# A decoder on one core: projection of the first attention in quarters and three units ahead, and another order of splits and additions in the last stage

## The reference

```
q, k = rope(x @ wq), rope(x @ wk)      # 16 and 4 heads of 128
v = x @ wv                             # 4 heads of 32
attn = softmax(q @ k.T / sqrt(128) + mask)
out = (attn @ v) @ wo
```

```
output = silu(x @ Ws1) * (x @ Wsg) @ Ws2
p = softmax(x @ gate_w + gate_b); top3 = top_k(p + biases, 3)
for e in range(7):
    output += (silu(x @ W1[e]) * (x @ Wg[e]) @ W2[e]) * w_e   # w_e: share of e in top3, or 0
```

## Time and profile before

| | us |
|---|---|
| median of 3 runs | 2308.58 (2304.91 to 2310.09) |
| profiled execution | 2314.31 |
| its span | 2312.2 |
| PE busy in the span | 1995.7 (86%) |
| DVE busy | 1452.0 (63%) |
| ACT busy | 1076.5 (47%) |
| POOL busy | 605.4 (26%) |
| mean granted TensorE clock | 0.939 |

### The profile page before, as it was taken

The page is one execution under the profiler, slowest core; times in us unless marked ns, Lnnn a source line. Parts: engine busy times, 40 slices in busy tenths (PEclk is TensorE's granted clock), DMA queues, the critical chain, the costliest instruction groups (busy, mean ns, idle before and its releaser), DMA issues. The chain is left out here.

```text
span 2312.2 us, 32930 instructions
## 1 busy us (share of the span) xinstructions
PE 1995.7 (86%) x11168; PEld 1201.7 (52%) x11168; DVE 1452.0 (63%) x2728; ACT 1076.5 (47%) x2150; POOL 605.4 (26%) x510
## 2 busy tenths in 40 slices
PE   6777776978999889996999999996698886699998
PEld 4454553446777567773545445453255543355553
DVE  5565565456775667766856667587699966445434
ACT  3555543222333323331635446371798893244332
POOL 3555520013332223320100101011644550132320
PEclk8999987988999889998999999997699998799999
DMA  4000003111110111104011010003700003467533
GB/s 134 24 24 1 1 1 114 37 48 46 46 45 0 58 36 46 45 0 133 21 30 43 19 36 18 0 1 65 175 1 2 1 1 109 136 184 179 145 72 88
DMA packets 95792, 125.26 MB, mean 54 GB/s; under 512 B 8926, under 2 KB 52254, under 8 KB 95662
## 3 DMA queue, kind: packets, MB, share of 16 engines
q1 hardware_dynamic: 88942, 107.79, 15.8%
q0 software_dynamic: 6720, 15.73, 3.6%
HBM read 101.68 MB, written 18.61 MB: 52 GB/s over the span
## 5 line engine op out<-in xcount | busy, mean ns | idle before, releaser
L1164 POOL TENSOR_TENSOR wl<-stage,wh 128x512 fp32r<-128x512 f32 x80 | 117.2, 1496 | 399.4 <-DVE wh L1155 399.4
L1423 POOL TENSOR_TENSOR Zl<-z,Zh 128x512 f16<-128x512 f32 x32 | 51.1, 1597 | 494.3 <-ACT Zh L1584 494.3
L1264 ACT ACTIVATE h<-PS,bup 128x512 f32<-128x512 f32 x64 | 44.2, 690 | 279.2 <-PE PS L79 279.2
L77 PE MATMUL PS<-XTh,wh 128*128 128x512 f16 x416 | 157.9, 380 | 0.5 <-DVE wl L1662 0.5
L78 PE MATMUL PS<-XTl,wh 128*128 128x512 f16 x416 | 157.9, 379 | 0.0
L79 PE MATMUL PS<-XTh,wl 128*128 128x512 f16 x416 | 157.7, 379 | 0.0
L2461 POOL TENSOR_TENSOR PTl<-P,PTh 128x512 f16<-128x512 f32 (+2 forms) x128 | 116.2, 918 | 124.6 <-ACT PTh L2633 124.5
L2632 ACT ACTIVATE P<-PS 128x512 f32<-128x512 f32 (+3 forms) x256 | 135.1, 528 | 21.7 <-PE PS L2558 19.8
L2633 ACT ACTIVATE PTh<-PS 128x512 f16<-128x512 f32 (+3 forms) x256 | 136.2, 532 | 0.0
L2648 DVE TENSOR_REDUCE M<-PS 128x1 f32<-128x640 f32 (+3 forms) x128 | 127.1, 1013 | 4.5 <-PE PS L2534 4.4
L2461 DVE TENSOR_TENSOR PTl<-P,PTh 128x512 f16<-128x512 f32 (+1 forms) x128 | 96.1, 756 | 50.0 <-ACT PTh L2633 48.7
(11 more groups left out here) (378 smaller groups left out, 5831.4 us busy)
## 6 DMA issues: line engine op xcount, KB each, us to landing
stage<-in_ffn_W SPq DMA_DIRECT2D x18, 1024.0 KB, 5.4
stage<-in_ffn_Wg SPq DMA_DIRECT2D x9, 1024.0 KB, 5.5
stage<-in_ffn_Wup SPq DMA_DIRECT2D x16, 512.0 KB, 3.9
stage<-in_ffn_Wdn SPq DMA_DIRECT2D x16, 512.0 KB, 3.6
wq<-in_attn_wq SPq DMA_DIRECT2D x4, 1024.0 KB, 5.5
C<-in_ctx SPq DMA_DIRECT2D x8, 512.0 KB, 8.8
stage<-in_ffn_Wsw SPq DMA_DIRECT2D x16, 256.0 KB, 3.6
stage<-in_attn_WV SPq DMA_DIRECT2D x16, 256.0 KB, 4.1
```

The costliest lines, as they stand in the source:

```text
L77: pe.matmul(out, a[0], b[0], start=start, stop=False, skip_group_check=True)
L1164: nc.gpsimd.tensor_tensor(piece(wl[q], ch), piece(st, ch), plain(piece(wh[q], ch)), ALU.subtract).then_inc(w_lo, 1)
```

## The change

In the first attention, `project(n)` becomes `project(n, k)`, a quarter of a tile. Each quarter (two, where a unit has two tiles to project) follows a score tile and its transpositions, for the tiles that unit u + 3 needs; before, whole tiles for unit u + 2 followed the fourth score tile. The first three units' tiles are projected ahead of the loop. ACT makes the high copies for unit u + 1 and the `halves` for unit u + 2 after exp 0 of unit u, the copies ahead of PTh and the halves behind it. DVE's `cosines` move behind the first maximum, with `outputs` for unit u - 2. POOL makes the low half of unit u + 1's tiles and then turns unit u + 2's. In the last stage the store of `rows` moves behind load 2; split 2 moves ahead of the router's exp on ACT and of `place` on DVE; splits 3 and 4 move between the shared expert's blocks; `name` and its matmuls move one block forward; two additions move ahead of split 5.

```diff
--- before.py
+++ after.py
@@ -766,7 +766,7 @@
         @block.sync
         def _(sp):
             for n in range(LOADS):
-                if n == 2:
+                if n == 3:
                     sp.dma_start(c.rows.rearrange("(t p) d -> p t d", p=P), c.X[:]).then_inc(rows_stored, 16)
                 e, i = divmod(n, 3)
                 need(sp, w_ready, n - 1)
@@ -888,8 +888,8 @@
             route.counts(pe)
             shared_up(0, 1, 0)
             shared_up(0, 2, 0)
+            route.name_tokens(pe)
             shared_up(0, 3, 0)
-            route.name_tokens(pe)
             pe.wait_ge(w_ready, 3)
             for q in range(QT):
                 shared_down(0, q, 0)
@@ -962,13 +962,14 @@
             split_hi(0)
             route.copy(act, 1)
             split_hi(1)
+            split_hi(2)
             route.exp(act)
-            split_hi(2)
             for m in range(KD):
                 silu(m, 2 * (m % 2))
                 shared_g(0, m)
-            for n in range(3, 6):
-                split_hi(n)
+                if m in (1, 2):
+                    split_hi(m + 2)
+            split_hi(5)
             x_high(0)
             for j in range(TILES):
                 silu(KD + j, 0)
@@ -1035,16 +1036,21 @@
             split_lo(0)
             split_lo(1)
             route.select(dve)
+            split_lo(2)
             route.place(dve, lambda: (g(0, 1), shared_low(0, 0)))
-            split_lo(2)
             for m in range(1, KD):
                 g(m, 2 * (m % 2) + 1)
                 shared_low(0, m)
-            route.name(dve)
+                if m == 1:
+                    split_lo(3)
+                if m == 2:
+                    route.name(dve)
+            split_lo(4)
             route.weigh(dve)
-            for n in range(3, 6):
-                split_lo(n)
-            for q in range(QT):
+            for q in range(2):
+                add_shared(0, q)
+            split_lo(5)
+            for q in range(2, QT):
                 add_shared(0, q)
             route.slot_weights(dve)
             x_low(0)
@@ -1792,7 +1798,7 @@
 
     def tiles(u):
 
-        if u >= N:
+        if not 0 <= u < N:
             return []
         first = u + u // REP + (1 if u % REP else 0)
         return [first, first + 1] if u % REP == 0 else [first]
@@ -1867,37 +1873,43 @@
         @block.gpsimd
         def _(pool):
             def rotate(n):
-                g, b, hh = tile(n)
-                q, u = n % 2, KVH * B * g + REP * b + hh - 1
-                hi, lo = (Kh[:, b, :], Kl[:, b, :]) if hh == 0 else (Qh[:, u % 2, :], Ql[:, u % 2, :])
+                q = n % 2
                 pool.wait_ge(a_half, 2 * n + 2)
                 nc.gpsimd.tensor_tensor(t2[:, q, :], t2[:, q, :], sin[:], ALU.mult).then_inc(r_sin, 1)
                 pool.wait_ge(r_sin, n + 1)
                 pool.wait_ge(a_cos, n + 1)
                 need(pool, r_lo, n - 1)
                 nc.gpsimd.tensor_tensor(r32[:, q, :], t1[:, q, :], t2[:, q, :], ALU.add).then_inc(r_sum, 1)
+
+            def low(n):
+                g, b, hh = tile(n)
+                u = KVH * B * g + REP * b + hh - 1
+                hi, lo = (Kh[:, b, :], Kl[:, b, :]) if hh == 0 else (Qh[:, u % 2, :], Ql[:, u % 2, :])
                 pool.wait_ge(r_hi, n + 1)
-                nc.gpsimd.tensor_tensor(lo, r32[:, q, :], hi, ALU.subtract).then_inc(r_lo, 1)
+                nc.gpsimd.tensor_tensor(lo, r32[:, n % 2, :], hi, ALU.subtract).then_inc(r_lo, 1)
 
             nc.gpsimd.memset(zero[:], 0.0).then_inc(zeroed, 1)
             nc.gpsimd.memset(Vh[:, :, :, DV:VW], XS).then_inc(ones_done, 1)
             nc.gpsimd.memset(Vl[:, :, :, DV:VW], 0.0).then_inc(ones_done, 1)
             pool.wait_ge(const_in, 48)
-            for u in range(N):
-                for n in tiles(u):
+            for u in range(-2, N):
+                for n in tiles(u + 1):
+                    low(n)
+                for n in tiles(u + 2):
                     rotate(n)
 
         @block.tensor
         def _(pe):
-            def project(n):
+            def project(n, k):
                 g, b, hh = tile(n)
-                pe.wait_ge(w_lo, (REP + 1) * g + hh + 1)
-                need(pe, a_half, 2 * (n - 1))
-                for k in range(KD):
-                    last = products(pe, c.PS[:, n % 2, :], (wh[:, g, hh, k, :], wl[:, g, hh, k, :]),
-                                    (c.XTh[:, k, b * S:(b + 1) * S], c.XTl[:, k, b * S:(b + 1) * S]),
-                                    start=(k == 0), stop=(k == KD - 1))
-                last.then_inc(a_done, 1)
+                if k == 0:
+                    pe.wait_ge(w_lo, (REP + 1) * g + hh + 1)
+                    need(pe, a_half, 2 * (n - 1))
+                last = products(pe, c.PS[:, n % 2, :], (wh[:, g, hh, k, :], wl[:, g, hh, k, :]),
+                                (c.XTh[:, k, b * S:(b + 1) * S], c.XTl[:, k, b * S:(b + 1) * S]),
+                                start=(k == 0), stop=(k == KD - 1))
+                if k == KD - 1:
+                    last.then_inc(a_done, 1)
 
             def scores(u, qt):
                 b = u // REP % B
@@ -1963,17 +1975,20 @@
                     last = products(pe, c.PS[:, 4 + t % 4, 0:KVH * DV], (c.XTh[:, k, tok], c.XTl[:, k, tok]),
                                     (wvh[:, k, :], wvl[:, k, :]), start=(k == 0), stop=(k == KD - 1))
                 last.then_inc(v_done, 1)
-            for n in tiles(0) + tiles(1):
-                project(n)
+            for n in tiles(0) + tiles(1) + tiles(2):
+                for k in range(KD):
+                    project(n, k)
             pe.wait_ge(v_lo, NT)
             pe.wait_ge(ones_done, 2)
             for u in range(N):
+                chunks = [(n, k) for n in tiles(u + 3) for k in range(KD)]
+                each = len(chunks) // QT
                 for qt in range(QT):
                     scores(u, qt)
                     if u > 0 and qt < NTU:
                         turn(u - 1, qt)
-                for n in tiles(u + 2):
-                    project(n)
+                    for n, k in chunks[each * qt:each * (qt + 1)]:
+                        project(n, k)
                 if u > 0:
                     values(u - 1)
             for j in range(NTU):
@@ -2024,21 +2039,20 @@
                 act.wait_ge(v_done, t + 1)
                 nc.scalar.activation(Vh[:, t, :, 0:DV], c.PS[:, 4 + t % 4, 0:KVH * DV].rearrange("p (g e) -> p g e", g=KVH),
                                      ACT.Copy, scale=1.0 / WS).then_inc(v_hi, 1)
-            halves(0)
-            halves(1)
-            rotated(0)
-            rotated(1)
-            halves(2)
+            for u in range(2):
+                for n in tiles(u):
+                    halves(n)
+                for n in tiles(u) if u == 0 else ():
+                    rotated(n)
             for u in range(N):
                 for qt in range(QT):
                     exp(u, qt)
-                    if qt == 2 and u + 1 < N:
-                        for n in tiles(u + 1):
-                            rotated(n)
+                    for n in tiles(u + 1) if qt == 0 else ():
+                        rotated(n)
                     if u > 0 and qt < NTU:
                         turned(u - 1, qt)
-                for n in tiles(u + 2):
-                    halves(n)
+                    for n in tiles(u + 2) if qt == 0 else ():
+                        halves(n)
             for j in range(NTU):
                 turned(N - 1, j)
             for t in range(NT):
@@ -2132,16 +2146,17 @@
                     maximum(u, qt)
                     if u > 0 and qt > 0:
                         turned(u - 1, qt - 1)
-                for n in tiles(u + 2):
-                    cosines(n)
-                if u > 0:
-                    outputs(u - 1)
-                for hh in {0: (0,), 1: (1,), 3: (2,), 4: (3,), 5: (4,)}.get(u % U, ()) if u < N - U else ():
+                    for n in tiles(u + 2) if qt == 0 else ():
+                        cosines(n)
+                    if u > 1 and qt == 0:
+                        outputs(u - 2)
+                for hh in {1: (0,), 2: (1,), 3: (2,), 4: (3,), 5: (4,)}.get(u % U, ()) if u < N - U else ():
                     weights(u // U + 1, hh)
                 if u == N - 3:
                     output_weights()
             for j in range(NTU):
                 turned(N - 1, j)
+            outputs(N - 2)
             z_part(0)
             z_part(1)
             outputs(N - 1)
```

## The result

The changed kernel takes 2270.44 us (median of four runs, 2268.35 to 2273.47), the kernel before on the same chip 2306.74 (2304.03 to 2310.09). The ratio is 0.9843 [0.9823, 0.9862]: 36.3 us faster. The forecast was 2262.5 in a range of 2244 to 2285, so the direction held and the gain of 46 was 10 too large.

A forecast was written before the change was run, and what follows sets the result against it. TensorE was taken to bound the attention loop, idle a quarter of the time behind DVE's PTl. Attention 34 + 7 - 4 = 37 us plus last stage 9 gave 46 off 2308.58: 2262.5 us, range 2244 to 2285.

The forecast's parts named there:

- The length of the units: First attention's loop: units of 6.4, 8.4, 9.3 and 6.8 us, 31.0 in four against 35.9; 34 us gained.
- the bank wait: First attention, units with u % 4 = 2: projection waits 2.7 us for ACT's halves to read its PSUM bank.
- The clock: First attention's loop: 4 us (0 to 10) charged against a sum made at full clock.
- rival 3: Attention: TensorE standing briefly in each unit could stay at 1.2 GHz, making the kernel slower, 2349 us; chance 4%.
- The ends of the loop: First attention: unit 1 starts about 3 us earlier, the end gives 4; 7 taken, between 0 and 8.
- Shared work of DVE and POOL: Attention loop: fifteen weight splits on DVE while POOL works could cost 0 to 13 us; 0 taken.
- The wait before products with V: One-tile units of the attention: about 0.6 us stays, derived from the last score tile's maximum and PTl.
- rival 1: Attention: halves before exp 1 in ACT's queue slow all one-tile units, bank wait 4.5; 2280 to 2285 us; chance 18%.
- The last stage: Up to the first routed tile: exp 5.0 us late, first addition 7.0 earlier; gain 9, bounds 2 and 12.
- the change of nothing (4): Whole kernel: no change within 0.2%; some 15 us won in the loop, 13 lost to DVE and POOL blocking; chance 3%.
- rival 5: Only the last stage fails, exp's 5 us not absorbed: 46 less 9, 2270 to 2274 us; chance 7%.
- Rival 2: Attention: waits all but go, four units approach 25.8 us; kernel at 2230 to 2245; chance 10%.

The follow-up runs named there:

- the mended projection: Changed kernel, but where u % 4 = 2 two quarters stand behind score tile 2 and two behind tile 3, none earlier; alone 2251.1 us, ratio 0.9744.
- the mended kernels: Changed kernel with late projection where u % 4 = 2 and exp ahead of split 2: 2245.42 us; also without a quarter behind tile 2 in other units: 2247.8.
- the mended version: Changed kernel with two quarters each behind score tiles 2 and 3 where u % 4 = 2, and exp ahead of split 2; 2245.42 us, ratio 0.9723.

## Why the prediction was right, and where it was wrong

*The length of the units* was right. Forecast 6.4, 8.4, 9.3 and 6.8 us; measured, where the clock stays up, 6.42, 8.33, 9.27 and 6.94. The wait before transpositions went, the bank wait came with 2.71 us (forecast 2.7), seven times, released by ACT's halves, in the unit named.

*The 10 us too many* (46 forecast, 36 measured) split up by the traces: 4.8 in the loop, 1.3 at its ends and 0.7 in the last stage, 6.8 in all. The other 3 lie within what the measurement can tell.

*The clock* is the mis-sized term. I charged 4 us for the loop. Four units last 10.94, 10.95, 12.20 and 10.64 in place of 9.27: 7.7 in the first profile, and with seven of seven about 4.5 more. The 28 units took 224.9 us in the first profile where the sum had 250.1 - 34 + 4 = 220, and 229.4 in the second. The reason for 4, that waits of 3 us remain only in every fourth unit, was true, but no row of mine priced a drawn-out unit. The price is 1.3 to 2.9 us for each, about half of the wait's own 2.71 or more. The trace of the kernel before has a lower one: six of its seven waits of 3.38 us have the low clock behind them, and in units with the same weight splits the four units from the wait at 182.66, with it, last 36.6 us, those from 111.19, without it, 35.3. There a part of the loss fell into time in which TensorE would have waited anyway: the next wait before transpositions, 0.83 us at 114.51, is gone at 186.60. The new order has little such time left. A summary of the clock, 0.95 before and 0.96 after, hid it: the share of slow time hardly fell, where the forecast had nearly full clock. The Trainium skill, "TensorE: Matmul & The Clock Gate", "A second HAM failure mode: psum-queue depth-cycling", stood behind rival 3, the kernel slower by its clock. The runs don't show a fall from cycling through banks alone: with the same banks in turn and waits of at most 1.43 us the granted clock is 1.00.

*The ends of the loop* were forecast at 7 and gave 5.7: unit 1 starts 2.9 us earlier (48.82 to 45.91, about 3 forecast), the tail is 2.8 shorter (4 forecast). One pair of traces doesn't fix this to better than 2 us: in the others with the new attention unit 1 starts at 44.1 to 46.3. A smaller slip is in the sum itself: 7 x 4.9 = 34, where the loop before was 250.1 and the four units gave 217, 33.

*Shared work of DVE and POOL*, costed at nothing, was nothing that shows: 28 units at the forecast lengths and the four drawn-out ones account for the loop within 0.3 us. DVE's split itself shows once the bank wait is mended: a unit with it is then 8.67 us instead of 7.65. How much of that comes from the two engines' sharing no run tells.

*The wait before products with V* had the right size by the wrong chain. I forecast 0.6 and derived it from the last maximum, which would begin 0.3 us behind its matmuls. It measured 0.48 to 0.69. But the maximum is ready and not waited for. DVE's timeline of the kernel after, unit 4:

```profile
76.10 0.56 DVE L2096 SCALAR_TENSOR_TENSOR PTl<-PS,PTh 128x384 f16<-128x384 f32 x1 [0.64 <-ACT PTh L2034]
76.58 0.55 DVE L2089 CUSTOM_DVE_ANT_0 Pr<-PS,mask 128x384 f32<-128x384 f32 x1
...
77.05 0.55 DVE L2096 SCALAR_TENSOR_TENSOR PTl<-PS,PTh 128x384 f16<-128x384 f32 x1
```

PTl 1 waits 0.64 for ACT, and maximum and PTl 2 follow without a gap; TensorE goes on at 77.66. The chain is rival 1's (halves ahead of exp 1), at the forecast's price, so that this figure came out right by luck. The kernel with no quarter behind tile 2 was made on the wrong chain and gained nothing. That a shorter stay of the halves in ACT's queue would shorten the wait wasn't tried.

*The last stage* was forecast at 9 and gave 8.3 in the profile, 5.3 to 12.2 alone. exp's delay was 5.9 instead of 5.0, the first addition 6.4 earlier instead of 7.0. From DVE's going on after exp to the first addition it is 38.6 us, where the sum had 39.3 + 5.7 - 6 = 39.0. The sum carried exp's delay in full, and rightly: with exp first again the stage is 5.5 to 7.0 us shorter. What the forecast didn't say is that the move could be left out: without it the first routed tile comes 13.6 to 15.3 us earlier than before, not 8.3. And the wait for the addition did not shrink to 2; it went, and 5.24 us came at the head of the same product. By the Trainium skill, "ScalarE: Activation LUTs", "What ACT_TABLE_LOAD costs", a drain of about 1.4 us would be added to each switch; the trace has 1.28 for the load at 1909.94 and exp right behind it at 1911.23, so no drain shows here. The load cost time for another reason: it stands behind a copy that waits 6.08 us for its transfer.

*Rivals.* The bank wait of 4.5 (rival 1) and the change of nothing (4) are excluded by the profile. Of rival 5 the condition came, exp's delay was not absorbed, but not its price: the other moves gave more than 9, and the stage still won 8.3. Rival 3's lasting fall didn't come, but part of its mechanism is what the forecast lacked. Rival 2, most waits gone, asked for a loop near four units in 26 us; the mended kernels, with 29.8, go less than a quarter of the way there from the 31.0 forecast, though their 2245 to 2248 lie near the upper end of its range, for they also have exp first.

Left open: why the same 2.71 us wait has the low clock behind it in four units of one execution, in five of others and in seven of yet others.

## What to carry to other kernels

Where in-order queues hand work round a loop, take the lead (how many units ahead, with the orders that belong to it) and the interleaving apart and price each. Here quarters alone moved the wait from one line to the next (0.9984), the lead with the new orders gave all that the whole change gave, and the mended version 64 us. Price a wait of TensorE with the clock it may cost behind it, the more so where little other waiting is left to take it up, and look for the bank that is taken too early. Put nothing that waits for a transfer ahead of a short instruction that another engine stands for.

## What the runs showed of the hardware

A TensorE wait of 2.71 us, once in about 31 us, was followed by matmuls of 0.63 instead of 0.38 us in four of seven cases, and in all seven when the same kernel was profiled again. The loop differed by 4.5 us between the two. In the kernel with whole tiles and the longer lead each of three waits of 2.47 us had the low clock behind it, and none of its waits of 0.93 to 1.45 us had. In the kernel before it was six of seven waits of 3.38 us. In the three kernels with the mended projection, with no wait above 1.43 us in the loop, the granted clock was 1.00 over 209 us. Their loop is 2.3 us a unit with the bank wait shorter than in one execution of the kernel after and 2.9 shorter than in the other; units that had kept their clock account for only 1.2 of it, and the rest is what the low clock cost.

ACT's table load is listed with 1.28 us, and exp begins 0.01 us behind its end (1909.94 and 1911.23).
